# The last stage of a two-layer graph kernel: per-node sums read by TensorE where they lie, without two staging copies

## Chip, cores and metric

The kernel runs on one core of a Trainium2 chip. The metric is the device time of one execution in microseconds (us). The time of the kernel before is the median of three runs. The profile is of one further execution.

## What is computed

The reference has 6250 nodes with 128 numbers each and 106250 edges, sorted by destination. Two layers follow one another, each with a layer norm and a ReLU ahead of it and a residual after it. Cut to what matters for the change, the second layer is:

```python
h = jnp.maximum(_layernorm(x), 0.0)
Wx = (h @ W.T).reshape(n, HEADS, HEAD_DIM)            # 4 heads of 32
e = leaky_relu(a_src . Wx[src] + a_dst . Wx[dst])
ex = jnp.exp(e - segment_max(e, dst)[dst])
denom = segment_sum(ex, dst)
out = segment_sum(ex / denom[dst] * Wx[src], dst)     # numerators over denominators
x = x + elu(out.reshape(n, 128))
```

The kernel keeps numerators and denominators apart until all edges are done, and divides once per node and head.

## The kernel before

Edges are worked in 208 groups of 512 for each layer. Each engine has its own program; semaphores order them. For each group TensorE sums products and weights by destination into PSUM (`segment_sums`, L1105), and ScalarE adds them into `acc` in SBUF (`merge`, L638, whose largest step is L659). `acc` holds [128 features, 2, nodes]: plane 0 the numerators, plane 1 the denominators, with nodes along the free dimension. After layer 1 the semaphore `L1["merged"]` counts to 208.

The **last stage** turns `acc` into the output in 13 batches: twelve of 512 nodes (4 tiles of 128) and one of 106. In the kernel before a batch b goes through these steps:

- ScalarE copies the numerators of the batch into `hn_row` (`numerators`, L740 to L745), and GpSimd the denominators into `hT` (`denominators`, L599 to L604). Both take their column from a register, b * 512. Each is free to overwrite its buffer (two of each) when TensorE has finished batch b-2 (`fin_psum`).
- TensorE (`turn_out`, L1230) waits for both copies. For each tile it transposes the numerators into `bank[u]` (L1238), and with one matmul against `head_pick`, which has 4 columns, it brings the 4 denominators of each node into `bank[2 + u]` (L1239). u is b modulo 2.
- VectorE (`divide`, L1037) takes the reciprocal of the denominators (L1044) and multiplies it onto the numerators (L1049), into `aggT`, which is the upper half of `ring_h`.
- ScalarE (`elu`, L729) makes relu(-y) (L735) and exp of its negative (L737) in `elu_e`.
- VectorE (`finish1`, L1055) makes max(y, 0) plus the residual (L1063, `pos`) and adds the exponential less one (L1070, `fin`).
- SyncE (`store_out`, L465) sends `fin` to the output (L470; the short last batch L468). `fin` has two buffers, and L1070 of batch b waits until the store of batch b-2 has landed.

The order on each engine is that of its `sweep` (L29): a stage list with lags, the first turns written out, then a hardware loop over two batches a turn with addresses and semaphore values in registers, then the last steps written out. On ScalarE the list is `[(2, elu), (0, numerators)]` (L748): elu of batch b-2, then the copy of batch b. On VectorE it is `[(1, divide), (2, finish1)]` (L1073): division of batch b, then the finish of batch b-1. GpSimd and SyncE have one stage each (L607, L473), TensorE has one (L1243).

Of the kernel before, what the change touches and what calls it, by code (L numbers as in the profile page):

```python
# [58 lines left out]
def gnn_kernel(nc, x_in, src_in, dst_in, ea_in, rule_in, w0_in, bias_in, beta_in, w1_in, a_in, out):  # L63
# [6 lines left out]
    GB = 4  # L70
# [24 lines left out]
    with ctx:  # L95
# [62 lines left out]
        inv_head = sb("inv_head", [P, GB * H])  # L158
# [90 lines left out]
        fin_num = sem("fin_num")  # L249
        fin_den = sem("fin_den")  # L250
# [51 lines left out]
        def offsets(eng, g):  # L302
            word = eng.value_load(packed[0:1, bass.ds(g, 1)], min_val=0, max_val=(WIN - P) * (1 + OFF + OFF * OFF))
            parts = (word % OFF, word // OFF % OFF, word // (OFF * OFF))
            return [0] + [nc.s_assert_within(eng.snap(x), 0, WIN - P, skip_runtime_bounds_check_because=
                                             "9 bits each, made by a min with WIN - P") for x in parts]


        @block.sync
        def _(sp):  # L310
# [154 lines left out]
            def store_out(b, u, use):  # L465
                sp.wait_ge(fin_out, b + 1)
                if isinstance(b, int) and b == NBAT - 1:
                    sp.dma_start(out[b * GE:N, :], fin[0:LAST, u, 0:D]).then_inc(out_stored[u], 16)  # L468
# [18 lines left out]
        def _(pool):  # L487
# [111 lines left out]
            def denominators(b, u, use):  # L599
                if later(b, 2):  # L600
                    pool.wait_ge(fin_psum, b - 1)
                apart(pool)
                w = LAST if isinstance(b, int) and b == NBAT - 1 else GE
                pool.tensor_copy(hT[:, u, 0:w], acc[:, 1, bass.ds(b * GE, w)]).then_inc(fin_den, 1)  # L604

            pool.wait_ge(L1["merged"], NG)
            sweep(pool, NBAT, 2, [(0, denominators)])  # L607


        @block.scalar  # L610
        def _(act):
# [117 lines left out]
            def elu(b, u, use):  # L729
# [3 lines left out]
                w = D if isinstance(b, int) and b == NBAT - 1 else GE  # L733
                r = LAST if isinstance(b, int) and b == NBAT - 1 else P
                act.activation(elu_e[0:r, u, 0:w], aggT[0:r, u, 0:w], ACT.Relu, scale=-1.0).then_inc(fin_neg, 1)  # L735
                act.wait_ge(fin_neg, b + 1)
                act.activation(elu_e[0:r, u, 0:w], elu_e[0:r, u, 0:w], ACT.Exp, scale=-1.0).then_inc(fin_exp, 1)  # L737


            def numerators(b, u, use):  # L740
                if later(b, 2):
                    act.wait_ge(fin_psum, b - 1)
                apart(act)
                w = LAST if isinstance(b, int) and b == NBAT - 1 else GE
# [7 lines left out]
        def _(dve):  # L752
# [284 lines left out]
            def divide(b, u, use):  # L1037
                last = isinstance(b, int) and b == NBAT - 1
                t = 1 if last else GB
                w, r = t * D, (LAST if last else P)  # L1040
# [4 lines left out]
                if later(b, 2):  # L1045
# [3 lines left out]
                dve.tensor_tensor(aggT[0:r, u, 0:w].rearrange("p (k d) -> p k d", d=HD),  # L1049
                                  bank[u][0:r, 0:w].rearrange("p (k d) -> p k d", d=HD),  # L1050
                                  inv_head[0:r, 0:t * H].rearrange("p (k a) -> p k a", a=1).to_broadcast([r, t * H, HD]),
# [3 lines left out]
            def finish1(b, u, use):  # L1055
                last = isinstance(b, int) and b == NBAT - 1
                t = 1 if last else GB
                w, r = t * D, (LAST if last else P)
                tiles = nodes[:, b * GB:b * GB + 1, :] if last else nodes[:, bass.ds(b * GB, GB), :]
                if later(b, 2):  # L1060
                    dve.wait_ge(fin_out, b - 1)
                dve.wait_ge(fin_y, b + 1)
                dve.scalar_tensor_tensor(pos[0:r, u, 0:w].rearrange("p (t d) -> p t d", d=D),  # L1063
                                         aggT[0:r, u, 0:w].rearrange("p (t d) -> p t d", d=D), 0.0, tiles[0:r],
                                         ALU.max, ALU.add).then_inc(fin_pos, 1)
                dve.wait_ge(fin_pos, b + 1)
                dve.wait_ge(fin_exp, b + 1)
                if later(b, 2):
                    dve.wait_ge(out_stored[u], 16 * use)
                dve.scalar_tensor_tensor(fin[0:r, u, 0:w], elu_e[0:r, u, 0:w], -1.0, pos[0:r, u, 0:w], ALU.add, ALU.add  # L1070
                                         ).then_inc(fin_out, 1)

            sweep(dve, NBAT, 2, [(1, divide), (2, finish1)])  # L1073
# [3 lines left out]
        def _(pe):  # L1077
# [152 lines left out]
            def turn_out(b, u, use):  # L1230
                last = isinstance(b, int) and b == NBAT - 1
                pe.wait_ge(fin_num, b + 1)
                pe.wait_ge(fin_den, b + 1)
                if later(b, 2):
                    pe.wait_ge(fin_y, b - 1)
                r = LAST if last else P
                for t in range(1 if last else GB):
                    pe.transpose(bank[u][0:r, t * D:(t + 1) * D], hn_row[:, u, t * P:t * P + r], ident[:, :])  # L1238
                    ins = pe.matmul(bank[2 + u][0:r, t * H:(t + 1) * H], hT[:, u, t * P:t * P + r], head_pick[:, :],  # L1239
# [3 lines left out]
            sweep(pe, NBAT, 2, [(1, turn_out)])  # L1243
# [25 lines left out]
```

## Times and profile before

| what | us |
|---|---|
| three runs | 2381.50, 2384.46, 2385.74 |
| median | 2384.46 |
| the profiled execution, own time | 2380.09 |
| its span, first to last instruction | 2378.3 |
| the last stage in it, from the end of the last L659 (2336.75) to the end | 41.5 |

Positions in the trace are in us from the start of the span. A row of the timeline has the start, the duration, the engine, the line and operation, the tensors, and in brackets how long the engine had idled and what released it. PE is TensorE, PEld its weight loads, DVE is VectorE, ACT is ScalarE, POOL is GpSimd, SPq is SyncE's queue. Several like instructions may stand in one row (x2).

### The profile page before, as it was taken

The numbers are of one execution on the slowest core, as the hardware profiler recorded it, in microseconds if no ns is written. First come the engines' busy times: TensorE is split into PE (matmuls) and PEld (weight loads), VectorE is DVE, ScalarE is ACT, GpSimd is POOL, SyncE is SP. The second block draws the span as 40 slices with busy tenths as digits, with TensorE's granted clock in tenths as the row PEclk, the third lists the DMA queues.
The fourth block names the chain that finished last, engine by engine and source line by source line (L and its number), as shares of the span: only waits on it lengthen the run. The fifth ranks groups of instructions, "written<-read, shape, count | busy, mean of one in ns | idle before, by whom it ended". The sixth has DMA issues, their size and how long they took to land.

```text
span 2378.3 us, 61655 instructions
## 1 busy us (share of the span) xinstructions
PE 1833.2 (77%) x14239; PEld 1681.1 (71%) x14240; DVE 2133.7 (90%) x4065; ACT 1335.0 (56%) x3451; POOL 1647.5 (69%) x1748
## 2 busy tenths in 40 slices
PE   0466666666666766666787989999999998999986
PEld 0466666666666666666566888888888888888886
DVE  5799999999999999999766888888888888898885
ACT  2366666666666666666223555555555555555554
POOL 3677777777777777777115777777777777777761
PEclk9999999999999999999757999999999999999985
DMA  5544444444444444443003333333333333333321
GB/s 126 143 131 129 131 129 130 131 127 124 130 127 132 129 130 131 129 130 108 3 15 87 61 59 60 59 58 59 59 59 58 58 59 59 59 59 58 59 52 54
DMA packets 338740, 214.13 MB, mean 90 GB/s; under 512 B 170817, under 2 KB 305197, under 8 KB 338686
## 3 DMA queue, kind: packets, MB, share of 16 engines
q0 software_dynamic: 53248, 112.57, 20.0%
q1 hardware_dynamic: 285438, 100.94, 16.6%
q8 instruction: 22, 0.36, 0.1%
q14 instruction: 32, 0.26, 0.0%
HBM read 201.32 MB, written 10.30 MB: 89 GB/s over the span
## 4 chain that ended last, share of the span: by engine, by line
POOL 44%; issue 20%; DVE 18%; PE 6%; DMA 6%; SPq 3%; ACT 2%; DVEq 1%; POOLq 1%; ACTq 0%
POOL msg L590 24%; POOL ring_h L559 20%; DVE seg_max L900 5%; DVE run_max L897 3%; DMA ring_h<-h_dram,meta_g 3%; DMA msg<-wx_dram,meta_g 3%; DVE sums L897 2%; DVE prod L935 2%; DVE msg L918 2%; PE sums L1156 1%; PE sums L1158 1%; SPq L457 1%; PE sums L1115 1%; DVE onehot L944 1%; DVE onehot L881 1%
## 5 line engine op out<-in xcount | busy, mean ns | idle before, releaser
L559 POOL DMA_INDIRECT ring_h<-h_dram,meta_g x832 | 809.6, 973 | 259.9 <-issue 258.4
L590 POOL DMA_INDIRECT msg<-wx_dram,meta_g x832 | 792.6, 953 | 264.6 <-issue 246.0
L1115 PE MATMUL sums<-onehot,prod 128*128 128x128 f32 x3328 | 697.3, 293 | 25.0 <-ACT acc L659 12.8
L1115 PE MATMUL sums<-onehot,wgt 128*128 128x128 f32 x3328 | 678.5, 288 | 0.0
L1115 PEld LDWEIGHTS sums<-onehot,prod 128*128 128x128 f32 x3328 | 538.5, 204 | 71.0 <-issue 68.1
L1115 PEld LDWEIGHTS sums<-onehot,wgt 128*128 128x128 f32 x3328 | 540.2, 204 | 0.0
L1124 PE MATMUL bank<-beta_ident,msg 128*128 128x128 f32 x1664 | 245.7, 292 | 341.9 <-DVE msg L918 341.8
L1124 PEld LDWEIGHTS bank<-beta_ident,msg 128*128 128x128 f32 x1664 | 205.5, 195 | 382.5 <-DVE msg L918 331.2
L659 ACT ACTIVATE acc<-sums 128x1022 f32 x414 | 423.7, 1023 | 0.0
L688 ACT ACTIVATE sums<-ring_h 128x512 f32<-128x512 f32 x208 | 125.1, 602 | 382.1 <-DMA ring_h<-h_dram,meta_g 381.9
L897 DVE TENSOR_TENSOR_SCAN sums<-flags,seg_max,bank 4x512 f32<-4x512 bf16 x207 | 264.0, 1275 | 5.8 <-PE bank L1211 4.4
L897 DVE TENSOR_TENSOR_SCAN run_max<-flags,run_max,bank 128x512 f32<-128x512 bf16 x207 | 263.5, 1273 | 0.0
L900 DVE TENSOR_TENSOR_SCAN seg_max<-flags,run_max 128x512 f32<-128x512 bf16 x208 | 254.6, 1224 | 7.1
L900 DVE TENSOR_TENSOR_SCAN seg_max<-flags,sums 4x512 f32<-4x512 bf16 x208 | 251.1, 1207 | 7.2
L651 ACT ACTIVATE carried<-acc,scale 128x2 f32 x414 | 120.9, 292 | 184.5 <-PE sums L1115 175.7
L1202 PEld LDWEIGHTS bank<-window,onehotT 128*128 128x128 f32 x1664 | 212.1, 200 | 4.1 <-ACT onehotT L721 2.9
L1202 PE MATMUL bank<-window,onehotT 128*128 128x4 f32 x1664 | 206.0, 247 | 2.8 <-DMA window<-wx_dram 1.3
L709 ACT ACTIVATE sums<-logit_d 128x16 f32<-128x16 f32 x208 | 39.0, 188 | 267.8 <-DVE logit_d L1022 266.0
L881 DVE TENSOR_SCALAR onehot<-iota_f,meta_g 128x128 f32<-128x128 f32 x832 | 180.4, 275 | 6.0 <-DMA meta_g<-meta 5.9
L918 DVE TENSOR_TENSOR msg<-msg,sums 128x512 f32<-128x512 f32 x208 | 141.0, 678 | 13.2 <-ACT sums L688 13.1
L1030 DVE TENSOR_TENSOR prod<-sums,msg 128x512 f32<-128x512 f32 x208 | 140.0, 673 | 4.8 <-PE sums L1115 4.5
L935 DVE TENSOR_TENSOR prod<-sums,msg 128x512 f32<-128x512 f32 x208 | 142.0, 683 | 1.8 <-ACT sums L676 1.8
(144 smaller groups left out, 2750.5 us busy)
## 6 DMA issues: line engine op xcount, KB each, us to landing
msg<-in_edge_attr SPq DMA_DIRECT2D x207, 256.0 KB, 3.1
flags<-flag_dram SPq DMA_DIRECT2D x52, 512.2 KB
ring_h<-h_dram,meta_g POOLq DMA_INDIRECT x832
msg<-wx_dram,meta_g POOLq DMA_INDIRECT x832
window<-wx_dram SPq DMA_DIRECT2D x832, 2.0 KB
wx_dram<-msg SPq DMA_DIRECT2D x13, 272.0 KB, 2.5
nodes<-in_x SPq DMA_DIRECT2D x4, 768.0 KB, 8.3
h_dram<-wgt SPq DMA_DIRECT2D x12, 256.0 KB, 2.4
```

The costliest lines, as they stand in the source:

```text
L559: pool.indirect_dma_start(hg[:, s % HRING, b, :], None, h_dram, bass.IndirectOffsetOnAxis(ap=meta_g[:, s, b:b + 1], axis=0)).then_inc(L0[" ...
L590: pool.indirect_dma_start(msg[:, s, b, :], None, wx_dram, bass.IndirectOffsetOnAxis(ap=meta_g[:, s, b:b + 1], axis=0)).then_inc(L1["gather ...
L659: act.activation(acc[:, :, bass.ds(node + 1, WIN - 1)], sums[:, par, :, 1:WIN], ACT.Copy).then_inc(k["merged"], 1)
L881: ins = dve.tensor_scalar(onehot[:, s, b, :], iota_f[:, :], key[:, b:b + 1], None, ALU.is_equal)
L897: dve.tensor_tensor_scan(run, flag[:, 0:GE], data, before, ALU.add, ALU.max).then_inc(k["scanned"], 1)
L900: dve.tensor_tensor_scan(seg_max[0:n, par, ::-1], flag[:, GE:0:-1], run[:, ::-1], -BIG, ALU.add, ALU.max).then_inc(k["scanned"], 1)
L918: dve.tensor_tensor(msg[:, s, :, 0:D], msg[:, s, :, 0:D], row_psum.rearrange("p (b d) -> p b d", b=GB), ALU.add).then_inc(L0["added"], 1)
L935: dve.tensor_tensor(prod[:, s % 2, :, :], wgt_psum.rearrange("p (b d) -> p b d", b=GB), msg[:, s, :, 0:D], ALU.mult).then_inc(L0["multipli ...
L1030: dve.tensor_tensor(prod[:, s % 2, :, :].rearrange("p b (h d) -> p b h d", h=H), head, msg[:, s, :, 0:D].rearrange("p b (h d) -> p b h d", ...
L1115: ins = pe.matmul(sums[:, 0, j, bass.ds(off, P)], what[:, slot, b, :], onehot[:, s, b, :], start=(b == 0), stop=(b == GB - 1), skip_group_ ...
L1124: ins = pe.matmul(bank[s % 2][:, b * P:(b + 1) * P], msg[:, s, b, 0:D], beta_ident[:, :], start=True, stop=True)
L1202: ins = pe.matmul(bank[2][:, b * H:(b + 1) * H], onehotT[:, s % 2, b * P:(b + 1) * P], window[:, s, b, :], start=True, stop=True)
```

## The change

The copies on ScalarE and GpSimd are left out. TensorE waits once for `L1["merged"]` and then uses slices of `acc` itself as weights, with addresses that are constants. The loops of the last stage are written out on all engines (`straight`), so registers, loop branches and the `nop` ahead of dynamic addresses go too. Numerators go round four banks, denominators round the four banks of `sums`, and the quotient round the four parts of `ring_h`, so that TensorE has to wait for the division of batch b-4 only. `inv_head` has two parts instead of one (64 bytes more in each partition, ahead of `pos`, `elu_e`, `fin`, `acc` and the buffers of the edge loops). `divide` drops its wait for the division before it, `finish1` its wait for the sum before it. The order of stages on VectorE stays; elu on ScalarE has no lag.

```diff
+def straight(count, stages):
+    for s in range(count + max(lag for lag, _ in stages)):
+        for lag, stage in stages:
+            if 0 <= s - lag < count:
+                stage(s - lag)
...
-        inv_head = sb("inv_head", [P, GB * H])
+        inv_head = sb("inv_head", [P, 2, GB * H])
...
 SyncE
-            def store_out(b, u, use):
+            def store_out(b):
...
-                    sp.dma_start(out[bass.ds(b * GE, GE), :].rearrange("(t p) d -> p t d", p=P),
-                                 fin[:, u, :].rearrange("p (t d) -> p t d", d=D)).then_inc(out_stored[u], 16)
-            sweep(sp, NBAT, 2, [(0, store_out)])
+                    sp.dma_start(out[b * GE:(b + 1) * GE, :].rearrange("(t p) d -> p t d", p=P),
+                                 fin[:, b % 2, :].rearrange("p (t d) -> p t d", d=D)).then_inc(out_stored[b % 2], 16)
+            straight(NBAT, [(0, store_out)])
...
 GpSimd
-            def denominators(b, u, use):
...
-                pool.tensor_copy(hT[:, u, 0:w], acc[:, 1, bass.ds(b * GE, w)]).then_inc(fin_den, 1)
-            pool.wait_ge(L1["merged"], NG)
-            sweep(pool, NBAT, 2, [(0, denominators)])
...
 ScalarE
+            def elu(b):
+                t, r = extent(b)
                 act.wait_ge(fin_y, b + 1)
+                if b >= 2:
                     act.wait_ge(fin_out, b - 1)
+                below = elu_e[0:r, b % 2, 0:t * D]
+                act.activation(below, ring_h[0:r, b % HRING, 0:t * D], ACT.Relu, scale=-1.0).then_inc(fin_neg, 1)
                 act.wait_ge(fin_neg, b + 1)
+                act.activation(below, below, ACT.Exp, scale=-1.0).then_inc(fin_exp, 1)
-            def numerators(b, u, use):
...
-                act.activation(hn_row[:, u, 0:w], acc[:, 0, bass.ds(b * GE, w)], ACT.Copy).then_inc(fin_num, 1)
-            act.wait_ge(L1["merged"], NG)
-            sweep(act, NBAT, 2, [(2, elu), (0, numerators)])
+            straight(NBAT, [(0, elu)])
...
 VectorE, divide
                 dve.wait_ge(fin_psum, b + 1)
-                if later(b, 1):
-                    dve.wait_ge(fin_y, b)
-                dve.reciprocal(inv_head[0:r, 0:t * H], bank[2 + u][0:r, 0:t * H]).then_inc(fin_inv, 1)
-                if later(b, 2):
-                    dve.wait_ge(fin_exp, b - 1)
-                    dve.wait_ge(fin_pos, b - 1)
+                dve.reciprocal(inv, sums[0:r, b % 2, b // 2 % 2, 0:t * H]).then_inc(fin_inv, 1)
+                if b >= HRING:
+                    dve.wait_ge(fin_exp, b - HRING + 1)
+                    dve.wait_ge(fin_pos, b - HRING + 1)
                 dve.wait_ge(fin_inv, b + 1)
...
 VectorE, finish1
-                if later(b, 2):
-                    dve.wait_ge(fin_out, b - 1)
                 dve.wait_ge(fin_y, b + 1)
...
                 dve.wait_ge(fin_pos, b + 1)
                 dve.wait_ge(fin_exp, b + 1)
+                if b >= 2:
+                    dve.wait_ge(out_stored[b % 2], 16 * (b // 2))
...
-            sweep(dve, NBAT, 2, [(1, divide), (2, finish1)])
+            straight(NBAT, [(0, divide), (1, finish1)])
...
 TensorE
-            def turn_out(b, u, use):
-                last = isinstance(b, int) and b == NBAT - 1
-                pe.wait_ge(fin_num, b + 1)
-                pe.wait_ge(fin_den, b + 1)
-                if later(b, 2):
-                    pe.wait_ge(fin_y, b - 1)
...
+            def turn_out(b):
+                t, r = extent(b)
+                if b >= HRING:
+                    pe.wait_ge(fin_y, b - HRING + 1)
+                for i in range(t):
+                    at = b * GE + i * P
+                    pe.transpose(bank[b % HRING][0:r, i * D:(i + 1) * D], acc[:, 0, at:at + r], ident[:, :])
+                    ins = pe.matmul(sums[0:r, b % 2, b // 2 % 2, i * H:(i + 1) * H], acc[:, 1, at:at + r], head_pick[:, :],
+                                    start=True, stop=True)
                 ins.then_inc(fin_psum, 1)
+            pe.wait_ge(L1["merged"], NG)
+            straight(NBAT, [(0, turn_out)])
```

## Rows read from the trace of the kernel before

**Rows 1.** Busy time by stretch: middle and end of the last stage.
```profile
core 0: us, PE busy (x) PEld busy (x) DVE busy (x) ACT busy (x) POOL busy (x), PEclk, DMA share, GB/s
2344.00:2369.50 25.50, 21.66 (x115) 20.94 (x114) 20.46 (x37) 16.47 (x29) 5.18 (x9) 0.50 0.33 93
```

**Rows 2.** Waits in the last stage: us in total, times, longest.
```profile
DVE inv_head L1044 <- PE bank L1239: 17.4, 8, 13.3
```

**Rows 3.** The chain that ended last, one turn: start, us, what.
```profile
2354.24 0.64 ACT elu_e L735
...
2355.44 0.62 ACT hn L745
...
2356.19 0.47 PE bank L1238
...
2358.61 0.27 DVE inv_head L1044
```

**Rows 4.** Timeline around the start of the last stage, ScalarE and TensorE.
```profile
2330.90 1.02 ACT L659 ACTIVATE acc<-sums 128x1022 f32 x1
...
2332.07 0.46 PE L1115 MATMUL sums<-onehot,prod 128*128 128x128 f32 x2 [2.05 <-ACT acc L659]
...
2335.73 1.02 ACT L659 ACTIVATE acc<-sums 128x1022 f32 x1
...
2337.65 0.45 PE L1238 MATMUL bank<-ident,hn 128*128 128x128 f32 x1 [2.80 <-POOL hT L604]
...
2339.77 0.45 PE L1238 MATMUL bank<-ident,hn 128*128 128x128 f32 x1
```

**Rows 5.** Timeline of VectorE, steps written out: batches 0 and 1.
```profile
2339.95 0.26 DVE L1044 RECIPROCAL inv_head<-bank 128x16 f32<-128x16 f32 x1 [13.27 <-PE bank L1239]
...
2342.08 0.26 DVE L1044 RECIPROCAL inv_head<-bank 128x16 f32<-128x16 f32 x1 [1.15 <-PE bank L1239]
2342.38 0.69 DVE L1049 TENSOR_TENSOR ring_h<-bank,inv_head 128x512 f32<-128x512 f32 x1
2342.99 0.68 DVE L1063 SCALAR_TENSOR_TENSOR pos<-ring_h,nodes 128x512 f32<-128x512 f32 x1
2343.70 0.69 DVE L1070 SCALAR_TENSOR_TENSOR fin<-elu_e,pos 128x512 f32<-128x512 f32 x1
```

**Rows 6.** Timeline of VectorE, steps written out: batches 10 to 12.
```profile
2369.56 0.26 DVE L1044 RECIPROCAL inv_head<-bank 128x16 f32<-128x16 f32 x1
2369.95 0.69 DVE L1049 TENSOR_TENSOR ring_h<-bank,inv_head 128x512 f32<-128x512 f32 x1
2370.56 0.68 DVE L1063 SCALAR_TENSOR_TENSOR pos<-ring_h,nodes 128x512 f32<-128x512 f32 x1
2371.27 0.69 DVE L1070 SCALAR_TENSOR_TENSOR fin<-elu_e,pos 128x512 f32<-128x512 f32 x1
2371.88 0.17 DVE L1044 RECIPROCAL inv_head<-bank 106x4 f32<-106x4 f32 x1
...
2375.07 0.29 DVE L1070 SCALAR_TENSOR_TENSOR fin<-elu_e,pos 106x128 f32<-106x128 f32 x1 [0.78 <-DMA out<-fin]
```

**Rows 7.** Timeline of ScalarE: second half of one elu.
```profile
2343.76 0.63 ACT L737 ACTIVATE elu_e<-elu_e 128x512 f32<-128x512 f32 x1
```

**Rows 8.** The chain that ended last, at the store of batch 10.
```profile
2371.99 0.05 SPq L470
...
2372.14 2.81 DMA out<-fin
```

**Rows 9.** Timeline, SyncE's queue: the last store.
```profile
2375.39 0.30 SPq L468 DMA_DIRECT2D out<-fin  x1
```

**Rows 10.** Busy time by stretch, columns as in rows 1: clock and TensorE's work.
```profile
1240.00:1250.00 10.00, 9.84 (x76) 9.01 (x75) 7.86 (x17) 9.70 (x25) 1.22 (x7) 0.96 0.37 113
...
2340.00:2342.00 2.00, 2.00 (x12) 1.96 (x11) 0.90 (x2) 1.00 (x2) 0.61 (x1) 0.50 0.00 0
```

**Rows 11.** Costliest groups, a VectorE step of the layer 1 loop.
```profile
L1030 DVE TENSOR_TENSOR prod<-sums,msg 128x512 f32<-128x512 f32 x208 | 140.0, 673 | 4.8 <-PE sums L1115 4.5
```

More of the change, by code:

```diff
@@ L463, in _ @@
             sweep_edges(sp, [(0, load1), (2, flags1)])
-            def store_out(b, u, use):
+            def store_out(b):
+                t, r = extent(b)
                 sp.wait_ge(fin_out, b + 1)
-                if isinstance(b, int) and b == NBAT - 1:
-                    sp.dma_start(out[b * GE:N, :], fin[0:LAST, u, 0:D]).then_inc(out_stored[u], 16)
-                else:
-                    sp.dma_start(out[bass.ds(b * GE, GE), :].rearrange("(t p) d -> p t d", p=P),
-                                 fin[:, u, :].rearrange("p (t d) -> p t d", d=D)).then_inc(out_stored[u], 16)
-            sweep(sp, NBAT, 2, [(0, store_out)])
+                if t == 1:
+                    sp.dma_start(out[b * GE:N, :], fin[0:r, b % 2, 0:D]).then_inc(out_stored[b % 2], 16)
+                else:
+                    sp.dma_start(out[b * GE:(b + 1) * GE, :].rearrange("(t p) d -> p t d", p=P),
+                                 fin[:, b % 2, :].rearrange("p (t d) -> p t d", d=D)).then_inc(out_stored[b % 2], 16)
+            straight(NBAT, [(0, store_out)])
             for u in range(2):
@@ L1034, in _, with divide @@
             sweep_edges(dve, [(6, products1), (3, logits1), (5, shift1), (4, maxima1), (0, one_hot1)])
-            def divide(b, u, use):
-                last = isinstance(b, int) and b == NBAT - 1
-                t = 1 if last else GB
-                w, r = t * D, (LAST if last else P)
+            def divide(b):
+                t, r = extent(b)
+                inv = inv_head[0:r, b % 2, 0:t * H]
                 dve.wait_ge(fin_psum, b + 1)
-                if later(b, 1):
-                    dve.wait_ge(fin_y, b)
-                dve.reciprocal(inv_head[0:r, 0:t * H], bank[2 + u][0:r, 0:t * H]).then_inc(fin_inv, 1)
-                if later(b, 2):
-                    dve.wait_ge(fin_exp, b - 1)
-                    dve.wait_ge(fin_pos, b - 1)
+                dve.reciprocal(inv, sums[0:r, b % 2, b // 2 % 2, 0:t * H]).then_inc(fin_inv, 1)
+                if b >= HRING:
+                    dve.wait_ge(fin_exp, b - HRING + 1)
+                    dve.wait_ge(fin_pos, b - HRING + 1)
@@ L1048, in divide @@
                 dve.wait_ge(fin_inv, b + 1)
-                dve.tensor_tensor(aggT[0:r, u, 0:w].rearrange("p (k d) -> p k d", d=HD),
-                                  bank[u][0:r, 0:w].rearrange("p (k d) -> p k d", d=HD),
-                                  inv_head[0:r, 0:t * H].rearrange("p (k a) -> p k a", a=1).to_broadcast([r, t * H, HD]),
+                dve.tensor_tensor(ring_h[0:r, b % HRING, 0:t * D].rearrange("p (k d) -> p k d", d=HD),
+                                  bank[b % HRING][0:r, 0:t * D].rearrange("p (k d) -> p k d", d=HD),
+                                  inv.rearrange("p (k a) -> p k a", a=1).to_broadcast([r, t * H, HD]),
@@ L1052, in divide, with finish1 @@
                                   ALU.mult).then_inc(fin_y, 1)
[L1055 to L1060, printed above, removed]
-                    dve.wait_ge(fin_out, b - 1)
+            def finish1(b):
+                t, r = extent(b)
+                pos_b = pos[0:r, b % 2, 0:t * D]
@@ L1062, in finish1 @@
                 dve.wait_ge(fin_y, b + 1)
-                dve.scalar_tensor_tensor(pos[0:r, u, 0:w].rearrange("p (t d) -> p t d", d=D),
-                                         aggT[0:r, u, 0:w].rearrange("p (t d) -> p t d", d=D), 0.0, tiles[0:r],
-                                         ALU.max, ALU.add).then_inc(fin_pos, 1)
+                dve.scalar_tensor_tensor(pos_b.rearrange("p (t d) -> p t d", d=D),
+                                         ring_h[0:r, b % HRING, 0:t * D].rearrange("p (t d) -> p t d", d=D), 0.0,
+                                         nodes[0:r, b * GB:b * GB + t, :], ALU.max, ALU.add).then_inc(fin_pos, 1)
@@ L1076, in _ @@
+                dve.scalar_tensor_tensor(fin[0:r, b % 2, 0:t * D], elu_e[0:r, b % 2, 0:t * D], -1.0,
+                                         pos_b, ALU.add, ALU.add).then_inc(fin_out, 1)
+            straight(NBAT, [(0, divide), (1, finish1)])
         @block.tensor
@@ L1228, in _ @@
             sweep_edges(pe, [(4, turn1), (1, onehotT1), (7, sums1), (2, targets1), (4, unturn1)])
-            def turn_out(b, u, use):
-                last = isinstance(b, int) and b == NBAT - 1
-                pe.wait_ge(fin_num, b + 1)
-                pe.wait_ge(fin_den, b + 1)
-                if later(b, 2):
-                    pe.wait_ge(fin_y, b - 1)
[L1236 to L1239, printed above, removed]
+            def turn_out(b):
+                t, r = extent(b)
+                if b >= HRING:
[4 more added lines that the diff above has]
+                    ins = pe.matmul(sums[0:r, b % 2, b // 2 % 2, i * H:(i + 1) * H], acc[:, 1, at:at + r], head_pick[:, :],
                                     start=True, stop=True)
                 ins.then_inc(fin_psum, 1)
-            sweep(pe, NBAT, 2, [(1, turn_out)])
+            pe.wait_ge(L1["merged"], NG)
+            straight(NBAT, [(0, turn_out)])
 _INS = ["x", "src", "dst", "edge_attr_128", "L0_gnn_phm_rule", "L0_gnn_W", "L0_gnn_bias", "L0_gnn_beta",
```

19 lines of the change are left out of this document (2 added, 17 removed).

## The prediction

> **What bounds the kernel now.** I began with the times: the profiled execution took 2380.09 us over a span of 2378.3, so 1.8 us lie around it. The change touches only what comes after the last merge into `acc`, which ends at 2335.73 + 1.02 = 2336.75 [rows 4], so 41.5 us of 2378.3 are open to it. Nothing that it removes runs earlier. I then read busy times in the middle of that stage [rows 1]: in 25.5 us TensorE is busy for 21.66, VectorE for 20.46, ScalarE for 16.47. No engine is full, so the pace comes from waits between engines. The list of waits says which: VectorE's reciprocal waited for TensorE's denominators eight times, 17.4 us in all, of which 13.3 is the wait for the first batch; 4.1 us are left over the steady part [rows 2].
>
> The chain shows the turn of the loop [rows 3]: relu of one batch on ScalarE at 2354.24, its exponential behind it, then the copy of a later batch at 2355.44, TensorE at 2356.19, the reciprocal at 2358.61, and from there to ScalarE again. ScalarE does the copy behind the elu of an older batch, and TensorE needs the copy. That circle, elu, copy, transposes, division, elu, sets the pace. Over all twelve steps from the first reciprocal (2339.95) to the thirteenth (2371.88) it is 31.93 / 12 = 2.66 us a batch [rows 5, 6].
>
> **The change, part by part.** A difference of 0.2%, 4.8 us, is about what a measurement of this kernel can tell from none.
>
> *Start.* Now TensorE starts at 2337.65, behind a ScalarE and a GpSimd copy. Without them it has to wait for the merge alone. What that costs is seen one group earlier: a merge started at 2330.90 and ended at 2331.92, and TensorE's matmul that waited for it began at 2332.07, 0.15 us on [rows 4]. So TensorE starts at 2336.75 + 0.15 = 2336.90, 0.75 us earlier, and the first reciprocal moves from 2339.95 to 2339.20. Its data are the same 128 x 512 numbers with the same weight loads, merely from `acc`; I take the same time for them. No row shows weights from `acc`; the sums' loads from `prod` and `wgt` show no price by buffer, so I take no change, with the bounds further down.
>
> *TensorE's pace.* Between batches 0 and 1, where nothing held TensorE, its first transposes are 2339.77 - 2337.65 = 2.12 apart [rows 4] and the reciprocals 2342.08 - 2339.95 = 2.13 [rows 5]. That is at the lower clock, 0.50 of full. The number of its instructions stays, so it can deliver every 2.13 us from 2339.20 on, batch 1 at 2341.33.
>
> *VectorE's pace.* Each batch has four instructions in the order reciprocal(b), product(b), pos(b-1), fin(b-1), as before. Where all steps are written out and nothing is late, starts are apart by: reciprocal to product 0.30, to pos 0.61, to fin 0.71 [rows 5], and fin to the next reciprocal 2371.88 - 2371.27 = 0.61 [rows 6]. This makes 2.23. From the batch on where the product has two more waits in front of it (those that guard the buffer it writes), the first distance is 0.39 instead of 0.30 [rows 6], and the sum is 2371.88 - 2369.56 = 2.32. Before, these waits are there from batch 2 on; with the change from batch 4 on. The waits that `divide` and `finish1` lose stand in other gaps of these same rows; I credit nothing for them, as the gaps of 0.61 are shorter than the instructions of 0.69 that they follow, so those waits are hidden.
>
> VectorE needs 2.23 to 2.32 and TensorE 2.13, so **VectorE becomes the bound**, by a small margin. Reciprocals start: batch 0 at 2339.20, batch 1 at 2341.33 (TensorE), batches 2, 3, 4 at 2343.56, 2345.79, 2348.02 (3 x 2.23), batch 12 at 2348.02 + 8 x 2.32 = 2366.58. Before, it was 2371.88: **5.30 us** less.
>
> *What lies beside.* ScalarE has two instructions a batch, 0.63 each [rows 7] (0.64 in the chain [rows 3]), 1.3 us of 2.3, and its result is wanted some 3.5 us after the product starts; it is not late. If the copies had stayed there, it would have 1.95 a batch. GpSimd's thirteen copies leave nothing behind. The stores: from the end of fin(10), 2371.27 + 0.69 = 2371.96, to landing, 2372.14 + 2.81 = 2374.95, it is 2.99 us [rows 6, 8]. fin(b) starts two periods after fin(b-2) started, that is 4.64 - 0.69 = 3.95 after it ended. 2.99 is less, so the stores hold nobody, with 0.96 to spare, until the end.
>
> *Four batches ahead.* TensorE gains only 0.10 to 0.19 us on VectorE a batch, some 1.8 us by batch 12, not even one batch. The depth of four is worth nothing by this; two would do.
>
> *End.* From the short reciprocal (2371.88) on the order is as before. fin(12) still waits for the store of batch 10. That store's address no longer comes from registers: SyncE's work on L470 at 2371.99 precedes the transfer at 2372.14 [rows 8], 0.18 after fin(10) ended, while the last store, which has a constant address, starts at 2375.39, 0.03 after the end of fin at 2375.36 [rows 6, 9]. This gives 0.15 less at most; of it I take 0.12, as the transfer piece of the chain includes its issue. After that 2.9 us of the last store are unchanged.
>
> *Sum.* 5.30 + 0.12 = 5.4 us off the profiled execution: 2380.09 - 5.4 = 2374.7. The ratio is 0.9977, and on the median it is 2384.46 - 5.4 = **2379.0 us**. I put the median and not the profiled time under it, since that execution was below all three runs.
>
> *Bounds.* If the two buffer waits, met long before, cost nothing, VectorE's period is 2.23 throughout, 8 x 0.09 = 0.7 more gain, 6.1. If every period were TensorE's 2.13, it is 2.66 x 12 - 2.13 x 12 + 0.75 + 0.12 = 7.2. Against it: the code is now straight and fetched once. Passing from loops to written-out steps shows no gap in VectorE's rows beyond 0.2 us [rows 6], and the nearest bound above is a gap of one DMA's latency, 2.99 us [rows 6, 8], once, which brings the gain to 2.4. Weights from `acc` could gain nothing or cost up to the margin between 2.13 and 2.32 for free; only beyond 0.19 a batch would they count. I take nothing for both, as the nearest rows show nothing.
>
> **The clock.** In 2340 to 2342 TensorE has work for 2.00 of 2.00 us, and had from 2337.65 on, yet the granted clock stays 0.50, 1.2 GHz; in 1240 to 1250, between the layers, it is busy for 9.84 of 10 with transposes and wider matmuls (`turn_h`, `layer_in`), and the clock is 0.96, mostly 2.4 GHz [rows 10]. With the change TensorE has no gaps for four batches, so it might rise. [...] For the sum it matters little: VectorE is the bound in either case. A faster TensorE only brings batch 1 sooner: reciprocal(1) could follow at 2339.20 + 2.13 / 2 = 2340.27, and 1.06 us more are gained, 6.5 in all.
>
> **Rivals.**
> 1. *TensorE's clock rises* from batch 1 on, as above: 2384.46 - 6.5 = 2378.0. For it: no gaps. Against it: 4 us without gaps did nothing before [rows 10].
> 2. *The stores become the pace.* 256 KB now go out every 2.3 us instead of 2.66. If a store takes over 3.95 from fin's end to landing, L1070 waits and VectorE with all behind it. At 4.7 the period is (0.69 + 4.7) / 2 = 2.7, and of the gain 0.75 + 0.12 is left: 2383.6, no change that can be told. Against it: 2.99 was measured right behind two other stores, and the engines' share is 0.33 [rows 1].
> 3. *A late fetch* of straight code, once: gain 2.4, 2382.1, again no telling difference.
> 4. *Slower, by the place of the buffers.* `inv_head` grows by 64 bytes a partition and pushes `acc`, `msg` and all buffers of the edge loops. If gathers or merges liked the old addresses better, each of 2 x 208 groups [rows 11] pays. It takes (4.8 + 5.4) / 416 = 25 ns a group to make the kernel slower by 0.2%; at 40 ns it is 2384.46 + 16.6 - 5.4 = 2395.7. Nothing in the trace speaks for it; nor can it exclude it.
> 5. *The change does not do what it says:* TensorE does not run four ahead. I count that as part of the forecast, since it changes no number.
>
> **Numbers.** Forecast 0.68, clock 0.08, stores 0.07, fetch or another small loss 0.12, buffers 0.05. The forecast's 5.4 us is only 0.6 over the 4.8 that can be told, and the three runs before scatter over 4.2 us, so about a quarter of its chance falls within 0.2%, as does a little of the clock's: faster 0.68 x 0.76 + 0.07 = 0.59; same 0.16 + 0.01 + 0.07 + 0.12 = 0.36; slower 0.05. The range runs from the bound of 7.2 with half of the scatter, 2384.46 - 7.2 - 2.1 = 2375.2, to rival 2 with 0.9 of it, 2384.5, which takes in rival 3.
>
> **What would show it.** TensorE's first transpose 0.15 us behind the last L659. Starts of L1044 2.13 apart once, 2.2 thrice, then 2.3, with no wait for TensorE after batch 1. L1070 waits for a DMA only in batch 12. PEclk 0.50. The stage takes 41.5 - 5.4 = 36.1 us. The forecast is wrong if VectorE's reciprocals wait for TensorE past batch 2, if L1070 waits for stores, or if the last L659 no longer ends near 2336.8.

## The result and the profile after

The changed kernel took 2377.02 us, median of 14 runs (2374.81 to 2379.16); the kernel before, run beside it, 2383.98, of 14. The ratio is 0.9976 with a 95% interval of 0.9968 to 0.9983. On 2383.98 that is 5.7 us less (4.1 to 7.6); the forecast was 5.4, 2379.0 us, and it holds. Two of the 14 runs before, 2420 and 2426 us, were in a slower state and the ratio leaves them out. The two medians differ by 7.0 us, inside the same interval. The interval excludes 1, but its upper end, 0.9983, does not clear the 0.2% that the prediction had asked for. The profiled execution after has a time of 2377.54 and a span of 2375.8.

The last stage can be measured far better than the whole: from the end of the last L659, at 2338.96 + 1.02 = 2339.98, to the end it is 2375.8 - 2339.98 = 35.82 us. It was 41.55. The timeline of the kernel after, ScalarE and TensorE at the start of the stage, beside [rows 4]:

```profile
2338.96 1.02 ACT L659 ACTIVATE acc<-sums 128x1022 f32 x1
...
2340.04 0.47 PE L1220 MATMUL bank<-ident,acc 128*128 128x128 f32 x1 [1.96 <-ACT acc L659]
...
2342.20 0.46 PE L1220 MATMUL bank<-ident,acc 128*128 128x128 f32 x1
```

TensorE starts 0.06 us behind the merge instead of 0.90, and the second batch follows 2.16 later. VectorE in the same kernel, beside [rows 5, 6]; the lines are now L1032 for the reciprocal, L1037 product, L1047 pos, L1054 fin:

```profile
2342.38 0.26 DVE L1032 RECIPROCAL inv_head<-sums 128x16 f32<-128x16 f32 x1 [14.04 <-PE sums L1221]
...
2344.51 0.26 DVE L1032 RECIPROCAL inv_head<-sums 128x16 f32<-128x16 f32 x1 [1.15 <-PE sums L1221]
...
2346.73 0.25 DVE L1032 RECIPROCAL inv_head<-sums 128x16 f32<-128x16 f32 x1
2347.02 0.69 DVE L1037 TENSOR_TENSOR ring_h<-bank,inv_head 128x512 f32<-128x512 f32 x1
...
2367.39 0.25 DVE L1032 RECIPROCAL inv_head<-sums 128x16 f32<-128x16 f32 x1
2367.78 0.69 DVE L1037 TENSOR_TENSOR ring_h<-bank,inv_head 128x512 f32<-128x512 f32 x1
2368.38 0.68 DVE L1047 SCALAR_TENSOR_TENSOR pos<-ring_h,nodes 128x512 f32<-128x512 f32 x1
2369.10 0.69 DVE L1054 SCALAR_TENSOR_TENSOR fin<-elu_e,pos 128x512 f32<-128x512 f32 x1
2369.71 0.17 DVE L1032 RECIPROCAL inv_head<-sums 106x4 f32<-106x4 f32 x1
...
2372.22 0.29 DVE L1054 SCALAR_TENSOR_TENSOR fin<-elu_e,pos 106x128 f32<-106x128 f32 x1 [0.39 <-DMA out<-fin]
```

Only the first two reciprocals wait for TensorE. From the first to the thirteenth it is 27.33 us, where it was 31.93. The reciprocal is 0.29 ahead of the product in batch 2 and 0.39 in batch 11. In the list of waits of the stage the circle is gone:

```profile
DVE inv_head L1032 <- PE sums L1221: 15.2, 2, 14.0
ACT elu_e L735 <- DVE ring_h L1037: 14.8, 13, 3.4
```

The clock stayed down, with TensorE busy the whole time (stretches of the kernel after, columns as in [rows 1]):

```profile
2350.00:2360.00 10.00, 10.00 (x58) 10.00 (x58) 9.29 (x18) 5.75 (x10) 0.00 (x0) 0.50 0.42 129
```

The two spans differ by 2.5 us only, though, 2378.3 and 2375.8. The stage began at 2339.98 and not at 2336.75, for 3.23 us were lost ahead of it: -5.73 + 3.23 = -2.5. The last experiments find where.

### The profile page after: what moved, and what is told of

It is laid out like the page before. It is cut to its first block, busy times and chain, and to the rows that moved or that the text cites. A ratio compares the mean times of both kernels' runs of the same rounds, so it can differ in the third digit from the quotient of the medians.

```text
span 2375.8 us, 61417 instructions
## 1 busy us (share of the span) xinstructions
PE 1833.6 (77%) x14239; PEld 1681.2 (71%) x14240; DVE 2133.2 (90%) x4065; ACT 1328.4 (56%) x3438; POOL 1640.5 (69%) x1735
## 3 DMA queue, kind: packets, MB, share of 16 engines
q1 hardware_dynamic: 285438, 100.94, 16.6%
## 4 chain that ended last, share of the span: by engine, by line
POOL 51%; issue 21%; DVE 9%; DMA 8%; PE 6%; ACT 2%; SPq 1%; POOLq 1%; DVEq 0%; ACTq 0%
POOL ring_h L570 27%; POOL msg L601 24%; DMA ring_h<-h_dram,meta_g 5%; DMA msg<-wx_dram,meta_g 3%; DVE sums L888 2%; DVE seg_max L891 2%; PE sums L1099 2%; PE sums L1140 1%; PE sums L1142 1%; DVE onehot L872 1%; DVE prod L1021 1%; ACT sums L688 1%; ACT acc L659 1%; PE bank L1165 0%; DVE fin L1054 0%
## 5 line engine op out<-in xcount | busy, mean ns | idle before, releaser
L659 ACT ACTIVATE acc<-sums 128x1022 f32 x414 | 423.6, 1023 | 0.0
```

What stands on the lines that cost most here:

```text
L659: act.activation(acc[:, :, bass.ds(node + 1, WIN - 1)], sums[:, par, :, 1:WIN], ACT.Copy).then_inc(k["merged"], 1)
```

## The experiments

Twelve kernels ran. Each has one profiled execution; in it I read the stage from the end of the last L659, and three parts: from there to the first reciprocal, from the first to the thirteenth, and from there to the end. All in us; "last four" is from the end of the fifth last L659 to the end of the last, ahead of the stage.

| kernel | stage | to first reciprocal | first to 13th | 13th to end | last four |
|---|---|---|---|---|---|
| before | 41.55 | 3.20 | 31.93 | 6.42 | 18.4 |
| after | 35.82 | 2.40 | 27.33 | 6.09 | 22.5 |
| a_again (after, once more) | 35.76 | 2.39 | 27.31 | 6.06 | 23.8 |
| b_place | 41.58 | 3.20 | 31.91 | 6.47 | 23.8 |
| b_inplace | 36.51 | 1.64 | 27.92 | 6.95 | 22.0 |
| a_copies | 40.21 | 3.13 | 31.01 | 6.07 | 21.0 |
| a_depth2 | 34.61 | 1.40 | 27.16 | 6.05 | 22.0 |
| a_pe_less | 35.93 | 2.59 | 27.32 | 6.02 | 22.4 |
| a_pe_more | 36.85 | 2.60 | 28.14 | 6.11 | 22.2 |
| a_dynstore | 35.96 | 2.40 | 27.31 | 6.25 | 23.8 |
| a_pool2 | 41.24 | 1.41 | 33.01 | 6.82 | 21.7 |
| a_trim | 34.85 | 2.39 | 26.53 | 5.93 | 18.9 |
| a_warm | 33.76 | 1.41 | 26.32 | 6.03 | 16.9 |
| a_best | 32.96 | 1.40 | 25.54 | 6.02 | 16.6 |

### The same kernel again, and the place of the buffers alone (a_again, b_place)

```diff
 b_place, on top of the kernel before
-        inv_head = sb("inv_head", [P, GB * H])
+        inv_head_2 = sb("inv_head", [P, 2, GB * H])
+        inv_head = inv_head_2[:, 0, :]
```

> The changed kernel once more, beside the kernel with only the place changed on the same chip. Stage 35.8 (35.5 to 36.1), ratio 0.9976 (0.997 to 0.998). Rival that part of the 14 runs' difference came from the chip: nearer to 0.999.

> The kernel before; only inv_head is made 64 bytes a partition longer, which moves all buffers behind it. Theory that the place is worth nothing: ratio 1.000 within 0.0015. Rival that it carries part of the gain (the medians differ by 7 us where the stage gives 5.7): 0.999 or less; or that it costs: over 1.001.

a_again: ratio 0.9976 (0.9966 to 0.9986), stage 35.76. b_place: ratio 1.0001 (0.9992 to 1.0011), stage 41.58. Both ran on one chip in turn. The gain repeats, and 64 bytes of shift are worth nothing that shows. The slower rival 4 falls.

### Reads in place alone (b_inplace)

```diff
 on top of the kernel before; the loops of ScalarE, VectorE and SyncE stay
-            sweep(pool, NBAT, 2, [(0, denominators)])
-            sweep(act, NBAT, 2, [(2, elu), (0, numerators)])
+            sweep(act, NBAT, 2, [(0, elu)])
-                pe.wait_ge(fin_num, b + 1)
-                pe.wait_ge(fin_den, b + 1)
-                    pe.transpose(..., hn_row[:, u, t * P:t * P + r], ident[:, :])
+                    pe.transpose(..., acc[:, 0, at:at + r], ident[:, :])
-            sweep(pe, NBAT, 2, [(1, turn_out)])
+            pe.wait_ge(L1["merged"], NG)
+            straight(NBAT, [(0, turn_out)])
```

> The kernel before with one part of the change: TensorE reads acc in place with constants, the copies go; loops on ScalarE, VectorE and SyncE stay, with two buffers. The last stage (end of the last L659 to the end) was 41.5 us before and is 35.8 after; first to thirteenth reciprocal 31.9 and 27.3. Theory that the copies in the circle carry the gain: 28.2 between the reciprocals, stage 36.9 (36.5 to 37.4). Rival that loop overhead carries it: over 39.

TensorE's loop had to be written out here too, and elu lost its lag of two batches. 28.2 between the reciprocals was expected, 27.92 measured; no wait for TensorE after the second batch, as in the kernel after. The stage, 36.51, is at the edge of what was expected, but it began at a higher clock: the first reciprocal came at 1.64 and not 2.40. With 2.40 it would be 37.3. So reading in place takes 4.3 of the 5.7 us. The rest, 1.45, stays with the programs of ScalarE, VectorE and SyncE that this kernel keeps: 0.6 between the reciprocals, which are 2.31 and 2.42 apart in turn against 2.32, and 0.9 at the end, where the store of batch 10 took 3.28 us instead of 2.28.

### Written out, with the copies back (a_copies)

```diff
 on top of the kernel after
+            def numerators(b):
+                if b >= 2:
+                    act.wait_ge(fin_psum, b - 1)
+                w = LAST if b == NBAT - 1 else GE
+                act.activation(hn_row[:, b % 2, 0:w], acc[:, 0, b * GE:b * GE + w], ACT.Copy).then_inc(fin_num, 1)
+            act.wait_ge(L1["merged"], NG)
+            straight(NBAT, [(2, elu), (0, numerators)])
 (denominators on GpSimd likewise; TensorE waits for both and reads hn_row and hT)
```

> The changed kernel, all written out, but with the two copies back (same engines, same order, two buffers). Theory: the circle elu, copy, transposes, division is back at 2.6 us a batch and the start is 0.8 later: stage 41.0 (40.4 to 41.5). Rival that loops carry the gain: 36 to 38.

40.21, slightly under the range, and far from the rival. The circle is back; among the waits in the stage of this kernel:

```profile
DVE inv_head L1050 <- PE sums L1241: 17.6, 7, 13.2
PEld bank L1240 <- ACT hn L754: 7.6, 7, 3.0
PE bank L1240 <- ACT hn L754: 4.1, 6, 0.8
```

The reciprocals are 2.32 and 2.99 apart in turn. From the other side the split is the same: 40.21 - 35.82 = 4.4 for the copies, 41.55 - 40.21 = 1.3 for writing out, of which 0.9 lie between the reciprocals and 0.35 at the end. In b_inplace the programs that stayed cost 0.6 between the reciprocals, so the parts do not add up exactly. I had not expected the 0.9.

### The depth (a_depth2)

```diff
-                if b >= HRING:
-                    pe.wait_ge(fin_y, b - HRING + 1)
+                if b >= 2:
+                    pe.wait_ge(fin_y, b - 1)
```

> The changed kernel; TensorE waits for the division of batch b-2 instead of b-4. Theory: TensorE has a lead of under one batch, so nothing moves: stage 35.8 (35.5 to 36.1), reciprocals over 27.3. Rival that the depth is used: over 0.5 more.

27.16 between the reciprocals; the whole stage is even 1.2 shorter, 34.61. That is not the depth: 1.0 of it is the first reciprocal at 1.40 instead of 2.40, again the clock, and the rest is the second reciprocal, 1.96 behind the first instead of 2.13. The depth of four isn't used.

### TensorE with less and with more to do (a_pe_less, a_pe_more)

```diff
 a_pe_less
+                    if b < HRING or i == 0:
                         pe.matmul(sums[0:r, b % 2, b // 2 % 2, i * H:(i + 1) * H], acc[:, 1, at:at + r], head_pick[:, :], ...)
 a_pe_more
+                    for _ in range(2 if i == 0 else 1):
                         pe.transpose(bank[b % HRING][0:r, i * D:(i + 1) * D], acc[:, 0, at:at + r], ident[:, :])
```

> The changed kernel with TensorE's work cut: from batch 4 on the denominators of tiles 2 to 4 of each batch are left out (their reciprocals take what is there), about 1.5 instead of 2.13 us a batch. Theory that VectorE is the bound from batch 2 on: reciprocals over 27.3 as after, stage 35.8. Rival that TensorE holds a part: up to 5 less.

> The changed kernel with the first transpose of each batch made twice, 0.31 us more for TensorE, 2.44 a batch at the lower clock. Theory: the margin of 0.19 under VectorE's 2.32 is passed and TensorE becomes the bound: reciprocals over 11 x 2.44 + 2.3 = 29.1, first one 0.3 later, stage 37.9 (37.5 to 38.3; 1.0 less if the stage starts at the full clock). Rival (VectorE's margin is larger or the clock rises with more work): reciprocals over 27.3.

a_pe_less leaves out three quarters of the denominators from batch 4 on, so only its times mean something. Nothing moves: 27.32. TensorE now waits for VectorE four times. With more, the reciprocals are 2.35 apart from the first batch on, 28.14 in all, stage 36.85: longer, but less than expected. The price was wrong, not the bound. The second transpose of the same weights cost 0.22, not 0.31. The profile joins the two in one row (timeline, TensorE, of a_pe_more); their weight loads too stand in one row of two, so that one was saved is not shown, and why the second is cheaper stays open:

```profile
2344.72 0.67 PE L1221 MATMUL bank<-ident,acc 128*128 128x128 f32 x2
2345.18 0.43 PE L1222 MATMUL sums<-head_pick,acc 128*128 128x4 f32 x2
2345.47 0.45 PE L1221 MATMUL bank<-ident,acc 128*128 128x128 f32 x1
```

2.13 + 0.22 = 2.35, just over VectorE's 2.32, and the pace is TensorE's 2.35. At 2.35 TensorE sets the pace, at 2.13 it did not, so the margin is about as small as forecast.

### The store's address (a_dynstore)

```diff
 SyncE's program of the kernel before on top of the kernel after
-            straight(NBAT, [(0, store_out)])
+            sweep(sp, NBAT, 2, [(0, store_out)])
```

> The changed kernel with SyncE's stores in the old loop, addresses from a register. After the change fin(12) started 2.43 us after fin(10) had ended, before it was 3.11. Theory that the register address makes the store later: 3.1 again, and the stage 0.3 to 0.7 longer, 36.1 to 36.5. Rival that a store's latency just scatters: between 2.4 and 3.1, not tied to the form.

The theory holds for a small part only. fin(12) started 2.58 after the end of fin(10), where it was 2.43 after and 3.11 before. The register address is worth 0.15, the work ahead of the transfer. The transfer itself took 2.28 as after. The chain of this kernel, and of the kernel after, at the store of batch 10:

```profile
2368.66 0.05 SPq L480
...
2368.80 2.28 DMA out<-fin
```

```profile
2369.82 2.28 DMA out<-fin
```

It was 2.81 before [rows 8], 2.80 in b_place and 3.28 in b_inplace. What these three have in common, and none of the eight with 2.28 or 2.29 (after, a_again, a_dynstore, a_copies, a_depth2, a_pe_less, a_pe_more, a_warm), is a packet of the instruction queue in that moment. DMA queues of the kernel before, 2372 to 2375:

```profile
q1 hardware_dynamic: 528, 0.26, 31.0%
q14 instruction: 1, 0.01, 1.3%
```

In the kernel after the last such packet came between 2364.8 and 2365.8, as one store ended (4 packets of it) and before the next began to move, and from 2370 to 2374 there was none. So in the kernels that keep VectorE's and ScalarE's loops a packet falls near the end, and in the written-out ones none does. That the packet delays the store is read from eleven traces; no run moved it alone, and these three kernels have other things in common too.

### Two guard waits and a buffer (a_trim)

```diff
-                if b >= HRING:
-                    dve.wait_ge(fin_exp, b - HRING + 1)
-                    dve.wait_ge(fin_pos, b - HRING + 1)
...
-                if b >= 2:
+                if 2 <= b < NBAT - 1:
                     dve.wait_ge(out_stored[b % 2], 16 * (b // 2))
+                to = diff[0:r, 0, 0:D] if b == NBAT - 1 else fin[0:r, b % 2, 0:t * D]
```

> The changed kernel without the two waits ahead of the product that guard the buffer of batch b-4 (VectorE itself has waited for the same counts before), and with a buffer of its own for fin(12), so that it waits for no store. Theory that two long met waits cost 0.09 us: reciprocals 2.22 apart throughout, 26.6 in all instead of 27.3. Rival that the 0.09 come from elsewhere: 27.3. For the end: fin(12) starts about 0.35 earlier, but in all runs so far the end came 4.1 to 4.3 after fin(11) ended unless code was fetched then; theory that the last store queues behind store 11: still 4.1. Rival that fin(12) sets the end: 3.8.

26.53 between the reciprocals, 0.29 from reciprocal to product throughout: both waits, met long before, had cost 0.1 a batch. The end of the kernel came 4.11 after the end of fin(11), as after (4.17), though fin(12) now ended 3.58 before the end instead of 3.29. So fin(12) does not set the end, and the buffer gives nothing. That the last store queues behind store 11 fits, but no row shows the queueing itself. The timeline of a_trim, VectorE:

```profile
2357.12 0.25 DVE L1032 RECIPROCAL inv_head<-sums 128x16 f32<-128x16 f32 x1
2357.40 0.69 DVE L1034 TENSOR_TENSOR ring_h<-bank,inv_head 128x512 f32<-128x512 f32 x1
2358.01 0.68 DVE L1044 SCALAR_TENSOR_TENSOR pos<-ring_h,nodes 128x512 f32<-128x512 f32 x1
2358.72 0.69 DVE L1052 SCALAR_TENSOR_TENSOR fin<-elu_e,pos 128x512 f32<-128x512 f32 x1
2359.33 0.25 DVE L1032 RECIPROCAL inv_head<-sums 128x16 f32<-128x16 f32 x1
```

### VectorE relieved by GpSimd (a_pool2)

```diff
 on VectorE
-                dve.scalar_tensor_tensor(pos_b..., ring_h..., 0.0, nodes..., ALU.max, ALU.add).then_inc(fin_pos, 1)
 on GpSimd
+                pool.tensor_scalar(y_pos, y, 0.0, None, ALU.max).then_inc(fin_max, 1)
+                pool.wait_ge(fin_max, b + 1)
+                pool.tensor_tensor(pos_b..., y_pos..., nodes..., ALU.add).then_inc(fin_pos, 1)
 and without the two guard waits
```

> The changed kernel with max(y, 0) plus residual moved from VectorE to GpSimd (two instructions, by rows of before 0.6 and 1.28 us), and without the two guard waits. Theory: VectorE needs 1.5 us a batch, TensorE 2.13 at the lower clock is the bound: reciprocals over 25.5, stage 34.0 (33.7 to 34.6), 1.8 better than the change. Rival: GpSimd at 2.1 a batch is itself too late and fin waits for it: 35 to 37.

A clear miss: stage 41.24, ratio 1.0007 (0.9994 to 1.0019), the whole gain of the change lost. Groups of its last stage:

```profile
L617 POOL TENSOR_SCALAR hT<-ring_h 128x512 f32<-128x512 f32 x12 | 17.8, 1487 | 30.0 <-DVE ring_h L1049 30.0
L619 POOL TENSOR_TENSOR pos<-hT,nodes 128x512 f32<-128x512 f32 x12 | 15.2, 1268 | 1.0
L1062 DVE SCALAR_TENSOR_TENSOR fin<-elu_e,pos 128x512 f32<-128x512 f32 x12 | 12.7, 1062 | 10.6 <-POOL pos L619 10.6
```

I had priced GpSimd's maximum like its copy of the same size, 0.61. It takes 1.49, and did in batch 0 already, where VectorE had only a reciprocal and a product at hand. 1.49 + 1.27 = 2.76 a batch, 2.80 with what lies between: GpSimd is the bound. And `fin` on VectorE, which starts 0.07 after the maximum, takes 1.09 in most batches where it took 0.69. The Trainium skill, "SBUF — State Buffer", section "Who interferes with whom", says that a VectorE instruction with two inputs in SBUF contends with a GpSimd instruction that reads SBUF. `fin` has two such inputs; the rows fit, though the two don't exclude each other here for their full length.

### Idle gaps of TensorE filled (a_warm, a_best)

The 3.23 us lost ahead of the stage, and the first reciprocal at 1.40 or 2.40, looked like one cause. While the last groups of layer 1 drain, TensorE has 2 us of sums at the full clock, more at the lower one, and then waits about 2 us for the merge. Stretches of the kernel after, then of a_warm:

```profile
2320.00:2324.00 4.00, 2.92 (x16) 2.60 (x16) 2.50 (x5) 1.92 (x6) 0.00 (x0) 0.50 0.00 0
2324.00:2328.00 4.00, 3.60 (x16) 3.31 (x16) 0.36 (x1) 0.59 (x3) 0.00 (x0) 0.50 0.00 0
2336.00:2340.00 4.00, 2.08 (x13) 1.78 (x11) 0.00 (x0) 1.62 (x4) 0.00 (x0) 0.55 0.00 0
```

```profile
2320.00:2324.00 4.00, 4.00 (x37) 3.81 (x36) 2.38 (x5) 1.71 (x6) 0.00 (x0) 1.00 0.00 0
2328.00:2332.00 4.00, 3.41 (x29) 3.22 (x29) 0.00 (x0) 1.63 (x4) 0.00 (x0) 1.00 0.02 4
2340.00:2344.00 4.00, 4.00 (x45) 4.00 (x44) 3.86 (x9) 2.13 (x5) 0.00 (x0) 1.00 0.24 71
2348.00:2352.00 4.00, 3.43 (x20) 3.31 (x20) 3.80 (x7) 2.35 (x4) 0.00 (x0) 0.50 0.42 131
```

```diff
+            def keep_busy():
+                for _ in range(6):
+                    pe.matmul(bank[0][:, 0:P], ident[:, :], ident[:, :], start=True, stop=True)
 in segment_sums, ahead of the wait for the merge
+                if k is L1 and isinstance(g, int) and g >= NG - 5:
+                    keep_busy()
 and ahead of the last stage
+            keep_busy()
             pe.wait_ge(L1["merged"], NG)
```

> The changed kernel; TensorE makes six matmuls of the identity into an idle bank ahead of each of the last five waits for a merge of layer 1, and ahead of the last stage. The first reciprocal came 2.4 us after the last merge in most runs and 1.4 where the clock had been full then, by chance. Theory that TensorE's half idle time in the last groups lets its clock fall: the clock stays near 1.0 until the stage starts, first reciprocal at 1.4, groups of the last merges 4.1 us instead of up to 5.7 apart; 2 to 4 us faster than the change, ratio to before 0.9965 (0.996 to 0.9973). Rival that the matmuls come at half clock and delay the sums: slower than the change, 0.998 or more.

> The two before together: trimmed waits, own last buffer, matmuls in the idle gaps. If both theories hold: stage 34.1 (33.8 to 34.5), 3 to 4.5 us faster than the change, ratio to before 0.9962 (0.9957 to 0.9970). If only the trim holds: 0.9974.

a_warm: 2371.88 us, ratio to the kernel before 0.9947 (0.9931 to 0.9962), whose interval lies below that of the change run again (0.9966 to 0.9986). It does more than I had expected. The clock was 1.00 from 2320 to 2344, and the last three merges followed 4.01 apart each, where the kernel after had 5.81, 5.68 and 4.79. Timeline of a_warm, TensorE and ScalarE:

```profile
2329.86 1.54 PE L1091 MATMUL bank<-ident 128*128 128x128 f32 x12
...
2330.91 1.03 ACT L659 ACTIVATE acc<-sums 128x1022 f32 x1
2331.99 0.49 PE L1105 MATMUL sums<-onehot,prod 128*128 128x128 f32 x2 [0.59 <-ACT acc L659]
```

Here the six matmuls cost no time, since the wait for the merge ends last anyway. That holds for the last four of the six places. At the first one they took TensorE 2 us, and the sums, whose merge had ended at 2311.05, began at 2314.27; at the second the sums began 1.0 behind the end of their merge. The first place:

```profile
2310.03 1.02 ACT L659 ACTIVATE acc<-sums 128x1022 f32 x1
...
2312.23 2.25 PE L1091 MATMUL bank<-ident 128*128 128x128 f32 x12
2314.27 0.63 PE L1105 MATMUL sums<-onehot,prod 128*128 128x128 f32 x2
```

"Last four" does not count that. From the end of the sixth last L659 to the end of the last it is 24.9 us in a_warm and 24.1 in a_best, against 22.5 before, 27.4 after and 25.2 to 30.0 in the other kernels. So ahead of the stage the matmuls give less than the last column of the table suggests, and what they would give in the last four places alone was not run.

In the stage, batches 0 and 1 came 1.14 apart instead of 2.13; together with the first reciprocal this is 2.0 us. The rest of the stage is VectorE's and did not change. One run of a_trim, which has none of these matmuls, took 2371.61 us, no more than a_warm; its last groups were quick (18.9). So the gain of a_warm rests on the two intervals, from four runs on one chip and eleven on another, each beside the kernel before. a_best: 2372.99 us, ratio 0.9953 (0.9940 to 0.9965). Its stage is the shortest, 32.96, but over the runs it can't be told from a_warm; the scatter of the groups ahead is larger than the 0.8 us that the trimming gives. Both intervals lie below that of a_again, that of a_best by 0.0001 only. All of this costs TensorE 36 matmuls whose result nobody reads.

## Why the prediction was right

*What bounds.* The reading of the circle through ScalarE's copy held: with the copies back in written-out code the circle returned (a_copies), without them and with the loops it was gone (b_inplace).

*Start.* 0.15 behind the merge was forecast, 0.06 measured; the reciprocal at 2.45 against 2.40.

*TensorE's pace.* 2.13 held, from `acc` as from the copies.

*VectorE's pace.* From the first to the thirteenth reciprocal 27.38 was forecast (2366.58 - 2339.20) and 27.33 measured. The two periods, 2.23 and 2.32, are there in the batches where they were placed, and the cause given for the difference, two waits long met, was shown by a_trim. (ScalarE with the copies would have 3 x 0.63 = 1.9 us a batch, not 1.95; nothing rests on it.) That the pace is VectorE's by 0.19 was shown from both sides (a_pe_less, a_pe_more). That four batches of depth give nothing was shown by a_depth2.

*End.* This is the step with the wrong mechanism: "This gives 0.15 less at most; of it I take 0.12" and "After that 2.9 us of the last store are unchanged". From the thirteenth reciprocal to the end 6.30 was forecast, 6.09 measured. fin(12) came 0.68 sooner behind fin(10): 0.15 by the address (a_dynstore) and 0.53 by the transfer of store 10, 2.81 before and 2.28 after. But a_trim shows that fin(12) does not set the end. In thirteen of the fourteen kernels the end comes 4.10 to 4.33 after the end of fin(11) (4.22 before, 4.17 after; 4.74 in b_inplace). Of the 0.33 that was gained here, 0.28 is fin(11), which ends 1.92 after the thirteenth reciprocal and no longer 2.20. Timeline of VectorE, before and after:

```profile
2372.19 0.29 DVE L1049 TENSOR_TENSOR ring_h<-bank,inv_head 106x128 f32<-106x128 f32 x1
2372.67 0.69 DVE L1063 SCALAR_TENSOR_TENSOR pos<-ring_h,nodes 128x512 f32<-128x512 f32 x1 [0.18 <-DVE ring_h L1049]
```

```profile
2370.02 0.29 DVE L1037 TENSOR_TENSOR ring_h<-bank,inv_head 106x128 f32<-106x128 f32 x1
2370.22 0.68 DVE L1047 SCALAR_TENSOR_TENSOR pos<-ring_h,nodes 128x512 f32<-128x512 f32 x1
```

From the short product of batch 12 to pos(11) it was 0.48 and is 0.20. b_place and b_inplace, with VectorE's program of before, have 0.48 too, a_copies 0.21. The prediction had put the waits that `divide` and `finish1` lose at nothing, because they hide behind instructions of 0.69. The product of batch 12 takes 0.29 only, and there VectorE's new program gains 0.28. Whether the dropped waits or the constant addresses do it, no run separates.

*The clock.* It stayed at 0.50 in the middle of the stage, so rival 1 as told did not come. But the forecast missed that the clock at the stage's start is not fixed. Of the nine kernels that read in place and leave the gaps ahead as they are, three began it at a higher clock (1.40, 1.41, 1.64 to the first reciprocal). After the change TensorE was busy for all of 10 us (2350 to 2360) with transposes and 4-column matmuls, and the clock stayed at 0.50. In a_best the stage began at 1.00, and the clock went down within the same stream while TensorE had no gap:

```profile
2336.00:2337.00 1.00, 1.00 (x12) 1.00 (x12) 0.96 (x3) 0.97 (x2) 0.00 (x0) 0.87 0.00 0
2337.00:2338.00 1.00, 1.00 (x8) 1.00 (x7) 0.96 (x2) 0.97 (x3) 0.00 (x0) 0.50 0.00 0
```

In a_warm it went down too, but behind a wait of 0.96 us for VectorE. So work without gaps, of this kind, neither raised the clock nor held it. The Trainium skill, "TensorE: Matmul & The Clock Gate", section "Part 4: PE-mode transpose", says that the full clock does not engage for transposes, which do not count as TensorE being busy in the same way. The trace agrees, as far as this mix of transposes and matmuls goes.

*Stores, fetch, buffers.* Rival 2 did not come; L1054 waited for a store once, 0.4 us, in batch 12. Rival 3 did not come either, and by the traces it may be the other way round: the packet of the instruction queue near the end belongs to the kernels with loops. Rival 4 is measured at nothing (b_place).

*The whole.* 5.7 us by the ratio, 5.73 by the stage, 5.4 forecast. By the stage it is 0.80 at the start, 4.60 between the reciprocals and 0.33 at the end, where 0.75, 4.55 and 0.12 were forecast. That the ratio comes so near is partly luck, as its interval is 3.5 us wide. The single profiles differ by 2.5 only, since the clock in the last groups of layer 1 is down or up from execution to execution, for no cause that was found: "last four" ranges from 18.4 to 23.8 us over the twelve kernels that leave these gaps alone, and between before and b_place, whose times are the same, from one end of that range to the other. That is as large as the effect. A single pair of executions could have shown nothing or twice the gain.

## What to carry to other kernels

Where no engine is full, find the circle of waits; leaving out one step of it pays up to the next bound. Here the pace went from 2.66 to 2.28 us a batch, 0.38 for a copy of 0.62, as VectorE was the next bound. The new pace can be summed from start-to-start distances of written-out steps to a few hundredths of a us. A wait that was met long ago is not always free: two of them cost 0.1 us ahead of a dependent instruction here. Once a stage is bound by one engine, look at what is ahead of it: the clock that TensorE has in its idle gaps and behind them counts too, and filling them with idle matmuls took the ratio from 0.9976 to 0.9947, on two chips, about as much again as the change itself; a third of these matmuls was not free.

## What the hardware showed that I had not expected

- With gaps of 2 us in every 4, TensorE's clock in the last groups is 1.00 in some stretches and 0.50 in others, for no cause that was found (from 2328 to 2332 TensorE was busy for 2.02 us at 1.00 in the kernel before, for 1.96 us at 0.50 in a_pool2). With the gaps filled by matmuls it was 1.00 from 2320 us on into the last stage in a_warm, and the last groups took 4.01 us.
- The same stream of transposes and 4-column matmuls ran at 1.00 for 3 us at the start of the stage of a_best and then, without a gap, at 0.50.
- Two semaphore waits that were met long before cost 0.1 us between an instruction and one that needs its result (a_trim).
- A GpSimd maximum with a constant over 128 x 512 numbers takes 1.49 us where the copy took 0.61, and a VectorE instruction with two SBUF inputs beside it 1.09 instead of 0.69.
- The store of 256 KB took 2.28 or 2.29 us in eight kernels and 2.80 to 3.28 in the three in which one packet of the instruction queue fell into it; that the packet is the cause was not shown.
- The second of two transposes with the same weights costs 0.22 us at the lower clock, not 0.31.
